# A two-layer gated transformer kernel: another order of the products in the expert blocks, and of the first instructions of the prologue

## The reference

```python
# layer 0, attention: 16 heads of 8
wq, wk, wv = (q @ wq_w.T + wq_b), (k @ wk_w.T + wk_b), (v @ wv_w.T + wv_b)   # q = layernorm(x), k = v = ctx
attn = softmax(scores / sqrt(8)) @ wv
x = x + tanh(g_xattn[0]) * (attn @ wo_w.T + wo_b)
# layer 0, experts: the 2 best of 8 for each token, weights by softmax
h = einsum('nc,ech->enh', xf, W1); g = einsum('nc,ech->enh', xf, W2)         # 128 -> 256
y = einsum('enh,ehc->enc', silu(h) * g, W3)                                   # 256 -> 128
x = x + tanh(g_ffn[0]) * einsum('enc,ne->nc', y, combine)
# layer 1: another cross attention, another mixture of 8 experts
```

## Time and profile before

| | us |
|---|---|
| median of 3 runs | 508.64 (506.07 to 509.48) |
| the profiled execution, on the device | 504.81 |
| its span in the profile | 502.9 |
| TensorE busy | 460.3 |
| VectorE busy | 387.8 |
| ScalarE busy | 300.9 |
| GpSimd busy | 231.4 |

### The profile page before, as it was taken

The page is one execution under the profiler, slowest core; times in us unless marked ns, Lnnn a source line. Parts: engine busy times, 40 slices in busy tenths (PEclk is TensorE's granted clock), DMA queues, the critical chain, the costliest instruction groups (busy, mean ns, idle before and its releaser), DMA issues. The chain is left out here.

```text
span 502.9 us, 14460 instructions
## 1 busy us (share of the span) xinstructions
PE 460.3 (92%) x4462; PEld 373.9 (74%) x4462; DVE 387.8 (77%) x1684; ACT 300.9 (60%) x752; POOL 231.4 (46%) x320
## 2 busy tenths in 40 slices
PE   2478999999999999889999999989999999899997
PEld 1246877777777787677887887768888877777996
DVE  4557789999899878767688568767799986677973
ACT  2377877777777775455555665475535556453653
POOL 2322155666666445547300377543687871314420
PEclk9999999999999999999999999999999999999999
DMA  8801011111111110146664344220100221000011
GB/s 232 323 12 54 14 33 34 42 37 37 37 37 33 35 53 24 44 131 187 183 178 140 106 134 118 78 68 18 27 22 22 57 71 33 11 1 1 1 43 43
DMA packets 44126, 34.60 MB, mean 69 GB/s; under 512 B 5922, under 2 KB 40098, under 8 KB 43812
## 3 DMA queue, kind: packets, MB, share of 16 engines
q1 hardware_dynamic: 28884, 20.02, 13.1%
q0 software_dynamic: 4384, 8.93, 6.3%
q10 hardware_dynamic: 10800, 4.92, 3.5%
HBM read 21.85 MB, written 11.99 MB: 67 GB/s over the span
## 5 line engine op out<-in xcount | busy, mean ns | idle before, releaser
L473 POOL DMA_INDIRECT sent<-xr,rowu x60 | 59.0, 984 | 62.2 <-DVE rowu L1038 48.1
L489 POOL DMA_INDIRECT yg<-done,gidx x64 | 65.4, 1021 | 31.5 <-issue 15.6
L1257 DVE TENSOR_TENSOR act<-sil,bank 128x256 f32<-128x256 f32 x71 | 29.8, 420 | 26.8 <-ACT sil L693 25.7
L927 DVE TENSOR_REDUCE mx<-bank 128x8 f32<-128x512 f32 x64 | 41.1, 682 | 10.3 <-PE bank L1691 9.9
L455 POOL TENSOR_TENSOR ve<-mv,half 128x4 f32<-128x4 f32 (+1 forms) x40 | 8.8, 221 | 85.9 <-DVE mv L851 83.2
L693 ACT ACTIVATE sil<-bank 128x256 f32<-128x256 f32 x71 | 27.2, 383 | 35.3 <-PE bank L1864 34.4
L1880 PE MATMUL bank<-f0w_s,aT 128*128 x284 | 44.4, 279 | 0.8 <-DVE yb L1263 0.8
L634 ACT ACTIVATE Pr<-bank 128x512 f32<-128x512 f32 x64 | 34.7, 597 | 14.3 <-PE bank L1705 14.3
L640 ACT ACTIVATE PT<-bank 128x512 f32<-128x512 f32 x64 | 37.2, 609 | 4.5 <-PE bank L1654 4.1
L1691 PE MATMUL bank<-QK 64*64 64x256 f32 x512 | 36.7, 404 | 2.9 <-ACT QK L624 2.9
L1880 PEld LDWEIGHTS bank<-f0w_s,aT 128*128 128x128 f32 x284 | 37.2, 191 | 1.9 <-issue 1.2
(11 more groups left out here) (254 smaller groups left out, 1287.7 us busy)
## 6 DMA issues: line engine op xcount, KB each, us to landing
xb<-sent SPq DMA_DIRECT2D x71, 64.0 KB
done<-yb ACTq DMA_DIRECT2D x71, 64.0 KB
cT<-ctx_t_dram SPq DMA_DIRECT2D x16, 128.0 KB
f0w_s<-f_w_dram SPq DMA_DIRECT2D x1, 2048.0 KB, 10.5
Pr<-ctx_t_dram SPq DMA_DIRECT2D x8, 256.0 KB
QK<-ctx_tok_dram SPq DMA_DIRECT2D x8, 256.0 KB
out_dram<-xs SPq DMA_DIRECT2D x8, 256.0 KB, 2.3
xs<-x_dram SPq DMA_DIRECT2D x2, 512.0 KB, 6.8
```

What stands on the lines that cost most here:

```text
L473: nc.gpsimd.indirect_dma_start(sent, bass.IndirectOffsetOnAxis(ap=rowu[:, s, 2 * k + c:2 * k + c + 1], axis=0), rows[:, c, :], None).then_ ...
L489: nc.gpsimd.indirect_dma_start(yg[:, s, j, :], None, done[0:NG1 * P, :] if u < UG else done, bass.IndirectOffsetOnAxis(ap=gidx[:, s, j:j + ...
L927: nc.vector.tensor_reduce(mx[:, g, :], bank[SC_BANK[g]][:].rearrange("p (m k) -> p m k", k=L), AX, ALU.max).then_inc(S("a_max"), 1)
```

## The change

In the blocks, TensorE's step is: high product (waits only for `xbh`), wait for the load of `xb`, a word's read, shift and mask for the next step's expert, low product, `xb`'s transposition (waits for `xbl`), L1864 (waits for `b_ys`), W3, `act`'s transpositions. The expert of a step is kept and used again two steps later for W3 instead of being computed a second time.

In the prologue, VectorE sets the constant parts of `Vb`, `upb` and `run` first, then does the first norm; the rest of the small arithmetic follows as `prepare()` in u = -3. The sum of the biases is taken in u = -1, the split in u = 0. The groups of statistics are (1), (2), (3, 4), (5, 6, 7). TensorE starts with 11 products of the constant tile `onb` into bank 2 that nothing reads, and has 8 more behind the queries of unit 0 and 8 before the first transposition of maxima; its bias product stands in u = -2.

```diff
             first_group()
             v.wait_ge(ld_small, 80)
-            v.wait_ge(prep_act, 2)
-            nc.vector.tensor_scalar(bkm[:], ...
-            nc.vector.tensor_scalar(rsum[:, 1, :], ...
             for s in range(2):
                 last = nc.vector.tensor_copy(Vb[:, s, :, :, 16:18], ...
             last.then_inc(prep, 1)
-            nc.vector.tensor_copy(farb[:], farf[:]).then_inc(prep, 1)
             nc.vector.tensor_copy(upb[:], cst[:, C_UP:C_UP + P])
             nc.vector.tensor_copy(run[:], cst[:, C_RG:C_RG + E]).then_inc(S("r_run"), 1)
-            v.wait_ge(ld_attn, 64)
...
+            def prepare():
+                v.wait_ge(prep_act, 2)
...
+            def sum_biases():
                 v.wait_ge(prep_pe, 1)
                 nc.vector.tensor_tensor(rsum[:, 0, :], bank[7][:, 0:D], rowv[:, R_BO:R_BO + D], ALU.add).then_inc(prep_b0, 1)
-
+            def split_biases():
                 v.wait_ge(prep_b0, 1)
...
                 if isinstance(u, int) and u == -3:
-                    split_biases()
+                    prepare()
+                if isinstance(u, int) and u == -1:
+                    sum_biases()
                 if isinstance(u, int) and -2 <= u < 2:
-                    for group in ((1,), (2, 3), (4, 5), (6, 7))[u + 2]:
+                    for group in ((1,), (2,), (3, 4), (5, 6, 7))[u + 2]:
                         first_stats(group)
...
+                if isinstance(u, int) and u == 0:
+                    split_biases()
...
-            pe.wait_ge(prep, 7)
-            mm(bank[7][:, 0:D], bvb[:], wo_s[:], start=True, stop=True).then_inc(prep_pe, 1)
...
+                if isinstance(u, int) and u == 0 and j == 1:
+                    pe.wait_ge(prep_b0, 1)
...
+            def warm(n):
+                for _ in range(n):
+                    mm(bank[2][:], onb[:], onb[:].unsqueeze(1).to_broadcast([P, 4, P]), start=True, stop=True)
+
+            pe.wait_ge(fill, 8)
+            warm(11)
+            pe.wait_ge(ld_attn, 64)
...
+                if isinstance(u, int) and u == -1:
+                    warm(8)
...
+                if isinstance(u, int) and u == -2:
+                    pe.wait_ge(prep, 8)
+                    mm(bank[7][:, 0:D], bvb[:], wo_s[:], start=True, stop=True).then_inc(prep_pe, 1)
+                    warm(8)
...
+            chosen_by = {}
+
             def b_step(t):
                 q, first, last = t % TURN, min(t, TURN), NB - 1 - t
                 k = q % 2
+                wide = first >= 1 and last >= -1
+                if wide:
+                    e = chosen_by[t - 1] = expert(t, 1)
+                    high, low = (w[:, bass.ds(e, 1), :].rearrange("p e n -> p (e n)") for w in (f0w12_h, f0w12_l))
+                    pe.wait_ge(S("b_xts"), t)
+                    mm(bank[1 - k][:], xbh[:, 1 - k, :], high, start=True, stop=False)
                 if last >= 0:
                     pe.wait_ge(ld_b[q % 4], (t - q % 4) * 4 + 16)
-                    if first >= 1:
-                        pe.wait_ge(S("b_xls"), t)
-                    transposes("b_xt", bank[4], lambda c: xb[:, q % 4, :], 1)
-                if first >= 1 and last >= -1:
-                    e = expert(t, 1)
-                    pe.wait_ge(S("b_xls"), t)
-                    ...
-                    mm(bank[1 - k][:], xbh[:, 1 - k, :], high, start=True, stop=False)
-                    mm(bank[1 - k][:], xbh[:, 1 - k, :], low, start=False, stop=False)
-                    mm(bank[1 - k][:], xbl[:, 1 - k, :], high, start=False, stop=True).then_inc(S("b_hg"), 1)
                 if q == TURN // 2 and t + TURN // 2 <= NB + 2:
                     load_word(t // TURN + 1)
-                if first >= 2 and last >= -2:
-                    pe.wait_ge(S("b_act"), t - 1)
-                    if first >= 3:
-                        pe.wait_ge(S("b_ats"), t - 2)
-                    transposes("b_at", bank[6], lambda c: act[:, k, P * c:P * (c + 1)], 2)
+                if first >= 1 and last >= 0:
+                    pe.compute_val(expert(t + 1, 1))
+                if wide:
+                    mm(bank[1 - k][:], xbh[:, 1 - k, :], low, start=False, stop=False)
+                    pe.wait_ge(S("b_xls"), t)
+                if last >= 0:
+                    transposes("b_xt", bank[4], lambda c: xb[:, q % 4, :], 1)
+                if first >= 4:
+                    pe.wait_ge(S("b_ys"), t - 3)
+                elif first == 3:
+                    pe.wait_ge(S("a_x"), 1 + UA)
+                if wide:
+                    mm(bank[1 - k][:], xbl[:, 1 - k, :], high, start=False, stop=True).then_inc(S("b_hg"), 1)
                 if first >= 3:
-                    e = expert(t, 3)
+                    e = chosen_by[t - 3]
                     pe.wait_ge(S("b_ats"), t - 2)
-                    if first >= 4:
-                        pe.wait_ge(S("b_ys"), t - 3)
-                    else:
-                        pe.wait_ge(S("a_x"), 1 + UA)
                     for j in range(2):
                         last_mm = mm(bank[2][:, 0:D], aT[:, 1 - k, j, :], ...
                     last_mm.then_inc(S("b_y"), 1)
+                if first >= 2 and last >= -2:
+                    pe.wait_ge(S("b_act"), t - 1)
+                    transposes("b_at", bank[6], lambda c: act[:, k, P * c:P * (c + 1)], 2)
```

More of the change, by code:

```diff
@@ L882, in _ @@
             v.wait_ge(ld_small, 80)
-            v.wait_ge(prep_act, 2)
-            nc.vector.tensor_scalar(bkm[:], cst[:, C_KM:C_KM + HG], colv[:, BK:BK + 1], None, ALU.mult).then_inc(prep, 1)
-            nc.vector.tensor_scalar(rsum[:, 1, :], rowv[:, R_BQV:R_BQV + D], tg[:, 1:2], None, ALU.mult).then_inc(prep, 1)
             for s in range(2):
@@ L889, in _ @@
             last.then_inc(prep, 1)
-            nc.vector.tensor_copy(farb[:], farf[:]).then_inc(prep, 1)
             nc.vector.tensor_copy(upb[:], cst[:, C_UP:C_UP + P])
             nc.vector.tensor_copy(run[:], cst[:, C_RG:C_RG + E]).then_inc(S("r_run"), 1)
-            v.wait_ge(ld_attn, 64)
-            v.wait_ge(fill, 11)
-            nc.vector.tensor_copy(bvb[:], colv[:, BV:BV + 1].to_broadcast([P, P]))
-            nc.vector.tensor_scalar(wo_s[:], wo_s[:], tg[:, 0:1], None, ALU.mult).then_inc(prep, 1)
@@ L897, in _ @@
-            nc.vector.tensor_scalar(rowv[:, R_BO:R_BO + D], rowv[:, R_BO:R_BO + D], tg[:, 0:1], None, ALU.mult).then_inc(prep, 1)
-            for e in range(2):
-                last = nc.vector.tensor_copy(wv_eo[:, e, :].rearrange("p (h e d) -> p h e d", e=2, d=DH)[:, :, e, :],
-                                             wv_s[:].rearrange("p (h e d) -> p h e d", e=2, d=DH)[:, :, e, :])
-            last.then_inc(prep, 1)
-            nc.vector.tensor_copy(w1c[:].rearrange("p c m -> p (c m)")[:, 0:16:5], colv[:, W1S:W1S + 1].to_broadcast([P, 4])).then_inc(prep, 1)
@@ L903, in split_biases @@
-            def split_biases():
+            def prepare():
+                v.wait_ge(prep_act, 2)
+                nc.vector.tensor_scalar(bkm[:], cst[:, C_KM:C_KM + HG], colv[:, BK:BK + 1], None, ALU.mult).then_inc(prep, 1)
+                nc.vector.tensor_scalar(rsum[:, 1, :], rowv[:, R_BQV:R_BQV + D], tg[:, 1:2], None, ALU.mult).then_inc(prep, 1)
+                v.wait_ge(ld_attn, 64)
+                v.wait_ge(fill, 11)
+                nc.vector.tensor_copy(bvb[:], colv[:, BV:BV + 1].to_broadcast([P, P]))
+                nc.vector.tensor_scalar(wo_s[:], wo_s[:], tg[:, 0:1], None, ALU.mult).then_inc(prep, 1)
+                nc.vector.tensor_scalar(rowv[:, R_BO:R_BO + D], rowv[:, R_BO:R_BO + D], tg[:, 0:1], None, ALU.mult).then_inc(prep, 1)
+                for e in range(2):
+                    last = nc.vector.tensor_copy(wv_eo[:, e, :].rearrange("p (h e d) -> p h e d", e=2, d=DH)[:, :, e, :],
+                                                 wv_s[:].rearrange("p (h e d) -> p h e d", e=2, d=DH)[:, :, e, :])
+                last.then_inc(prep, 1)
+                nc.vector.tensor_copy(w1c[:].rearrange("p c m -> p (c m)")[:, 0:16:5], colv[:, W1S:W1S + 1].to_broadcast([P, 4])).then_inc(prep, 1)
+                nc.vector.tensor_copy(farb[:], farf[:]).then_inc(prep, 1)
@@ L1857, in b_step @@
-                    transposes("b_xt", bank[4], lambda c: xb[:, q % 4, :], 1)
-                if first >= 1 and last >= -1:
-                    e = expert(t, 1)
-                    pe.wait_ge(S("b_xls"), t)
-                    high, low = (w[:, bass.ds(e, 1), :].rearrange("p e n -> p (e n)") for w in (f0w12_h, f0w12_l))
-                    mm(bank[1 - k][:], xbh[:, 1 - k, :], high, start=True, stop=False)
-                    mm(bank[1 - k][:], xbh[:, 1 - k, :], low, start=False, stop=False)
-                    mm(bank[1 - k][:], xbl[:, 1 - k, :], high, start=False, stop=True).then_inc(S("b_hg"), 1)
```

## The result

The time after the change has a median of 508.12 us (20 executions, 506.29 to 510.12), that of the kernel before 506.35 us (20 executions beside them, 504.82 to 509.48). The ratio is 1.0033, 95% interval 1.0018 to 1.0048. So the change makes the kernel slower by a third of a per cent; the forecast was 0.4% faster. 508.12 lies inside the forecast's range, but the forecast started from the median of three runs, 508.64, which was 2.3 us high; the difference is what counts, and it has the wrong sign. Each execution also has a mean granted clock of TensorE, 1 for full speed throughout: it is 0.976 to 0.990 in the 20 executions after, with a median of 0.986; the kernel before, over the 84 executions beside the experiments, has a median of 0.997.

A forecast was written before the change was run, and what follows sets the result against it. The prediction took TensorE, busy 92% of the span, as the bound. Prologue -4.6 us and blocks +2.6 us summed to -2.0, taking the median of 508.64 us to 506.6, with a range of 499.8 to 510.5.

The forecast's parts named there:

- The loop over L1864, silu, `act`, `yb`: Blocks: L1864 waits for the previous step's `yb` copy, so a clean step takes 1.62 to 1.63 us against 1.47.
- The middle stretch: Blocks, 33 steps between the neighbour stages' work: 55.8 us forecast against 52.72 before, +3.1.
- the word: Blocks: reading a new word of experts, one step in eight, between high and low product; 0.5 us each, four in the middle.
- The 0.10 of the weight load: Blocks, L1864: its weight load no longer lies under the matmul before, adding 0.10 us to the step.
- Rival 1: Blocks: loop harmless, the arithmetic's gaps are the larger thing; steps 1.50 us, total 499.8 us; chance 0.17.
- Rival 2: Blocks: TensorE pulls the weight load ahead of the wait; loop 1.53 us, total 503.3 us; chance 0.12.
- Rival 4: Blocks: sequencer late at the low product, 0.12 us more in each of 71 steps, total 515 us; chance 0.10.
- The clock's 2.13: Prologue: unread products bring TensorE to 2.4 GHz by 16 us, saving 2.13 us from first transposition to next maximum.
- The third group: Unit 1: three groups of statistics before its maxima, for which TensorE already waits; costs 2.06 us.
- The attention loop is unchanged, so the shift is kept: Attention, after the prologue: the prologue's gain of 4.6 us was to last until the blocks.
- if the shift of the prologue isn't there when the blocks begin: Start of the blocks: sign that the forecast fails as a whole; they should begin at 200 us instead of 204.7.
- Rival 3: Prologue gives little: the 2.13 us gain from an earlier full clock fails; total 508.7 us, no change; chance 0.13.

The follow-up runs named there:

- e3: Kernel after with the wait for `b_ys` back in front of W3 instead of L1864; ratio 0.9969 to the kernel before, 504.43 us.
- e8: Kernel before with only the wait for the `yb` copy moved from W3 to in front of L1864; ratio 1.0106 to the kernel before, 511.18 us.
- e9: Kernel after without its 27 unread products of the prologue; ratio 1.0067 to the kernel before, 510.02 us.
- e1: Changed prologue of the kernel after with the old order in the blocks; ratio 0.999 to the kernel before, 505.17 us.
- e4: Kernel after with 12 more unread products in unit 1, before the transposition that waits; ratio 0.9979 to the kernel before, 504.54 us.
- e5: Kernel after with the `b_ys` wait back before W3, 12 unread products in unit 1, word's read behind W3; ratio 0.9875 to the kernel before, 499.77 us.
- e6: Changed prologue with 12 more unread products in unit 1 and the old order in the blocks; ratio 0.9907 to the kernel before, 501.45 us.
- e10: e5 with 5 more unread products in unit 0, before the transposition of its maxima; ratio 0.9876 to the kernel before, 500.33 us.
- e11: Kernel before with six unread products in unit 1, before the transposition of its maxima; ratio 1.0006 to the kernel before.
- e7: Kernel after with the statistics in the old groups (1), (2, 3), (4, 5), (6, 7); ratio 0.9973 to the kernel before, 505.21 us.

## Why the prediction was wrong, step by step

**Blocks: right in mechanism and nearly in size.** The loop over L1864, silu, `act`, `yb` was forecast at 1.62 to 1.63 and is 1.63. The middle stretch was to grow by 3.1 and grew by 2.55: the term that was too large is the word, 0.5 assumed, 0.36 measured (4 x 0.14 = 0.56). The first stretch was put at 0 and gave -0.6, the third at -0.5 and gave +0.4; both inside their bounds. Sum +2.6 forecast, +2.4 measured.

Two readings were wrong without harm to the sum. The 0.10 of the weight load was read from a high product "after a gap" (0.49), but that product takes as much without a gap (486 ns as the mean of all 71 before); the size came out right because the new place costs it, wait or no wait (e3, 477 ns). And "The clean steps are most of the 33"; by the starts of the `xbh` copies only 15 of the 33 before were 1.50 or shorter, the others 1.55 to 2.10.

Rival 1 (steps of 1.50) needed no loop; but e3, without the wait, has 1.48 and 1.57 by turns and a middle of 52.94, where the rival had 50.5. So its gain isn't there even without the loop. Rival 2 (1.53) fell: the load of L1896 starts 0.06 after the copy it waits for, not ahead of it. e8 shows the price of the wait in the old order: where its last product waited it took 0.50 (257.97) and 0.48 (261.67), where it didn't, 0.39 (263.60). The Trainium skill, TensorE: Matmul & The Clock Gate, section on the architectural detail of the array, lets loads pass matmuls in flight. A load that stands behind its own wait isn't such a case, and the traces of after and of e8 show it so (0.06 us behind the copy's end, and 0.26 and 0.33 us of waiting). Rival 4 (the sequencer late, 515) fell too: between the high and the low product TensorE has a gap only in steps with a word.

**Prologue up to unit 3: right.** First maximum 16.01 forecast, 15.60 measured (VectorE could begin on the tokens at 10.18, not at 10.74). The clock's 2.13 were 2.0 by e9. The third group cost 2.09 of waiting, forecast 2.06. At unit 3 the kernel was 5.0 ahead, forecast 4.6. The three-way split of the biases stayed hidden, with 0.30 us of VectorE's idle time left before the maxima at 30.61.

**The step that failed** is the last sentence of the part on the prologue: "The attention loop is unchanged, so the shift is kept". The shift was 5.0 us at unit 3 and 0.4 at unit 4. The forecast priced the longer wait of TensorE in unit 1 at its own length, 2.06, and not by what it does to the clock behind it, although in the paragraph before it had counted on the clock rising because pauses were filled. Term by term: for the third group +2.06 was assumed; measured were 2.09 and, by the clock, 4.6 more. The forecast named this outcome as the sign that would refute it ("if the shift of the prologue isn't there when the blocks begin"), but gave it no cause and no chance of its own.

That the wait is the cause is shown this far. The four kernels with a wait of 3.4 us in unit 1 (after, e1, e3, e9) all have the long fall in their profile, and it begins 2.8, 2.3 and 2.0 us into the wait in e1, e3 and e9 and 1.1 us behind it in the kernel after; they have a mean clock of 0.990 or less in 55 of 56 executions, the kernel before in 19 of 84. The four with the wait filled (e4, e5, e6, e10) have no such fall in their profiles; unit 4 comes 4.4 us ahead of the kernel before in e4, and the ratio drops by 0.5% (e4 against after) and 0.8% (e6 against e1), while filling a shorter wait gives nothing in the kernel before (e11). It isn't the only cause: e7 falls with no wait over 1.58 us in the 10 us before, and e4 still has a clock of 0.990 or less in 7 of 11 executions (its profiled one has 0.997, among its best), e6 in 5 of 9; whether those are one long fall or several short ones isn't shown.

The Trainium skill, TensorE: Matmul & The Clock Gate, section "HAM oscillation — how this bites in real kernels", describes a clock that falls again and again because the array waits for transfers between its bursts; here it was a wait for VectorE, once, and the row at 43 to 52 us of the kernel after (0.50) agrees that the matmuls behind such a wait can run at half clock. The Trainium skill, TensorE: Matmul & The Clock Gate, section "A second HAM failure mode: psum-queue depth-cycling", has the clock fall on short pauses between groups of matmuls too; no run here tests that for e7.

**Rival 3** gave 508.7 and 508.12 was measured. It was right in number only, by luck: it had the clock term fail at the start, and the clock term came. Anyone who compares medians alone would have taken it as confirmed; e9 tells the two apart.

**The sum, redone:** -5.0 (unit 3) + 4.6 (fall) + 2.4 (blocks) = +2.0 us, 0.4%, against 0.33% measured.

**What stays open:** why a fall lasts 10.24 or 13.66 us with TensorE busy from the end of the wait on; what sets off the fall in e7 and the short ones where the blocks begin and late in the third stage; how often e7 has its long fall; and whether e7's groups together with e3's wait and less filling would do as well as e5, which wasn't tried.

## What to carry to other kernels

When a change moves work of another engine ahead of a TensorE instruction, the price isn't the added wait alone: look whether the longest wait grows past what the kernel had before, and cost the matmuls behind it at both clocks. Moving one wait a few instructions up its queue can close a loop over three engines; add up that loop against the engine's own floor before believing that a reordering is free (here 1.63 against 1.47; moving the wait back gave 3.5 us in 71 steps). And follow a gain to its end: the same event of each later unit, in both traces, shows in which unit it is lost.

## What the hardware showed that was not expected

- The granted clock stayed at 1.2 GHz for 10.24 us (after, e7) or 13.66 us (e1, e3, e9), though TensorE had no pause in the 9 us of it looked at (busy 9.00 in after, e1 and e7).
- The column of the granted clock misses the slow start: in e9 it says 1.00 for the first 40 us, but the 16 score products at 14.07 take 1.99 us and the transposition at 17.88 takes 0.47, where the kernel after has 1.09 and 0.33. So e9's mean clock (0.983 in its profile) leaves out that loss.
- The clock fell with no wait over 1.58 us in the 10 us before (e7, at 31.32 us), and with none over 0.37 us in the 20 us before (e5, at 200.1 us). A wait of the same 1.58 us had no fall behind it in the profiles of before and e4.
- 12 products of 512 columns that nothing reads, 2.75 us of TensorE's time inside a wait, brought the blocks forward by 4 us; in the kernel before, whose wait was 1.34 us and whose profile has no fall, six of them gave nothing (1.0006).
- In e8 the last product takes 0.48 to 0.50 us where it waited and 0.39 where it didn't (257.97, 261.67, 263.60 us): its load is not covered any more. Without any wait it also takes 477 ns when it stands behind a transposition of 128 columns (e3). TensorE's idle column shows neither.
